# Spreading softmax divisors with two small matmuls, and moving a unit's projection beside its predecessor, in a one-core attention block

## What is computed

```python
q, k, v = heads(X @ Wq), heads(X @ Wk), heads(X @ Wv)      # 16, 8, 8 heads of 64
q, k = rope(q), rope(k)                                     # rotate by cos and sin
att = 50.0 * tanh(q @ k.T / 16 / 50.0)                      # causal mask, then softmax
y = softmax(att) @ v
x = layernorm(X + y @ Wo)
qx, s = per_token_quant_int8(x)                             # s = absmax / 127
x = layernorm(x + float16((qx @ weight.T) * s * w_scale + bias))
```

## Time and profile before

| | us |
|---|---|
| median of 3 runs | 1561.52 |
| lowest, highest | 1559.03, 1564.63 |
| the profiled execution | 1562.01 |
| its span, first to last instruction | 1560.3 |
| PE busy | 1317.1 (84%) |
| DVE busy | 1055.1 (68%) |
| ACT busy | 843.2 (54%) |
| POOL busy | 378.6 (24%) |

### The profile page before, as it was taken

How to read it: one execution, slowest core, us unless ns; L and a number is a source line. 1 busy time by engine, 2 the same in 40 slices (tenths; PEclk the granted TensorE clock), 3 DMA queues, 4 the chain that set the end, 5 groups by cost and what they waited for, 6 DMA issues and landing times.

```text
span 1560.3 us, 17566 instructions
## 1 busy us (share of the span) xinstructions
PE 1317.1 (84%) x5776; PEld 965.0 (62%) x5776; DVE 1055.1 (68%) x1334; ACT 843.2 (54%) x952; POOL 378.6 (24%) x477
## 2 busy tenths in 40 slices
PE   6489998988687999797777999979867799999564
PEld 5366776666465777575545677756655577776442
DVE  4377887763467888683456888877346788887354
ACT  4166676652227876673223877766222577788122
POOL 2231111112542111111344111111144311121354
PEclk9789999999898999899978999999999899999797
DMA  7755445366514344447621543546562344433531
GB/s 269 255 199 139 112 128 164 79 206 188 169 54 103 104 125 112 135 95 274 176 97 54 129 109 100 130 114 190 181 198 71 97 104 107 121 87 119 183 115 48
DMA packets 124715, 212.24 MB, mean 136 GB/s; under 512 B 28112, under 2 KB 70096, under 8 KB 120400
## 3 DMA queue, kind: packets, MB, share of 16 engines
q1 hardware_dynamic: 120016, 202.72, 45.7%
q10 hardware_dynamic: 4608, 8.39, 1.4%
HBM read 105.64 MB, written 38.27 MB: 92 GB/s over the span
## 4 chain that ended last, share of the span: by engine, by line
PE 48%; SPq 13%; DVE 13%; POOL 8%; DMA 7%; issue 7%; ACT 4%; POOLq 0%; DVEq 0%; ACTq 0%
PE ps L714 18%; PE ps L633 12%; PE ps L688 12%; SPq L467 7%; POOL y_raw L1256 4%; DMA rb<-r_scratch 3%; PE ps L736 3%; SPq L480 2%; PE ps L659 2%; SPq L413 1%; DVE prob_hi L1048 1%; DVE work_r L1038 1%; PE ps L756 1%; POOL rstd L1264 1%; DMA x_raw<-X_T 1%
## 5 line engine op out<-in xcount | busy, mean ns | idle before, releaser
L714 PE MATMUL ps<-prob_hi,v 128*65 128x512 f32 (+3 forms) x1280 | 419.4, 377 | 8.3 <-DVE prob_lo L1052 8.3
L688 PE MATMUL ps<-qk 128*128 128x512 f32 (+1 forms) x1280 | 328.2, 384 | 79.1 <-ACT probs L863 38.9
L863 ACT ACTIVATE probs<-ps 128x1024 f32<-128x1024 f32 x288 | 293.2, 1018 | 169.1 <-PE ps L688 167.7
L1052 DVE TENSOR_TENSOR prob_lo<-probs,prob_hi 128x1024 fp32r<-128x1024 f32 x288 | 356.6, 1238 | 9.9
L1246 POOL TENSOR_SCALAR_AFFINE_SELECT probs<-probs 128x256 f32<-128x256 f32 (+1 forms) x192 | 146.1, 768 | 829.6 <-ACT probs L868 829.6
L688 PEld LDWEIGHTS ps<-qk 128*128 128x128 f32 x1280 | 231.4, 195 | 146.1 <-issue 38.7
L868 ACT ACTIVATE probs<-probs 128x1024 f32<-128x1024 f32 x288 | 305.6, 1061 | 8.8
L633 PE MATMUL ps<-xT,w_ring 128*128 128x512 f32 x1152 | 292.5, 399 | 16.6 <-DVE xT L992 14.7
L1048 DVE CAST prob_hi<-probs 128x1024 fp32r<-128x1024 f32 x288 | 203.3, 706 | 136.5 <-POOL probs L1246 79.7
L633 PEld LDWEIGHTS ps<-xT,w_ring 128*128 128x128 f32 x1152 | 218.7, 192 | 63.4 <-DVE xT L992 15.3
L714 PE MATMUL ps<-prob_lo,v 128*65 128x512 f32 (+1 forms) x640 | 240.8, 376 | 0.0
(11 more groups left out here) (69 smaller groups left out, 982.2 us busy)
## 6 DMA issues: line engine op xcount, KB each, us to landing
qk<-work_r SPq DMA_DIRECT2D x256, 128.0 KB, 2.3
qk<-work_r SPq DMA_DIRECT2D x512, 64.0 KB, 2.0
y_scratch<-sums SPq DMA_DIRECT2D x256, 64.0 KB
wo<-wo_scratch SPq DMA_DIRECT2D x8, 2048.0 KB, 8.8
y_raw<-y_scratch SPq DMA_DIRECT2D x32, 512.0 KB, 4.3
rb<-r_scratch SPq DMA_DIRECT2D x128, 128.0 KB, 3.3
w_ring<-w_scratch SPq DMA_DIRECT2D x15, 1024.0 KB, 5.1
x_raw<-X_T SPq DMA_DIRECT2D x16, 512.0 KB, 7.2
```

Of the source, the lines that this page charges most:

```text
L688: mm = nc.tensor.matmul(scores[:, g % 2, col:col + REP * w].rearrange("p (h q) -> p h q", h=REP), qk[:, n % 2, i, 2 + part, keys], qk[:, n ...
L714: mm = nc.tensor.matmul(sums_ps[:, :, GQ - w:GQ], v[:, kt, v0:v0 + width], p[:, g % ring, col:col + REP * w].rearrange("p (h q) -> p h q", ...
L863: nc.scalar.activation(probs[:, g % PRING, :], scores[:, g % 2, :], ACT.Tanh, scale=SCORE_SCALE / SOFTCAP).then_inc(capped, 1)
L1052: nc.vector.tensor_tensor(prob_lo[:, g % PRING, :], probs[:, g % PRING, :], prob_hi[:, g % HRING, :].bitcast(F32), ALU.subtract).then_inc( ...
```

## The change

Four things move together.

1. Divisors. `invert` now also splits the inverse into a high and a low fp32r part (`inverse`, 128x32 each). `store_inverse` writes both parts to `r_scratch`, and `load_rows` loads, for one tile, four rows of 1024 numbers (two heads of a pair, high and low) onto four partitions of `rows`. A constant `spread` of 4x128 ones and zeros, made at the start, spreads them: `spread_rows` is two matmuls of 512 columns into PSUM banks 2 and 3. There is one `rows` buffer, so a tile's load waits for the spreading of the tile ahead. The broadcasting loads are gone.
2. Engines. `scale_y` goes from POOL to DVE (one 128x1024 multiply that reads PSUM), `split_y` from DVE to POOL (one 128x1024 subtraction). In the drain's lists ACT takes `keep_q` ahead of `round_y`, DVE takes `quantise` behind `rescale`, POOL takes both `inverse_std` ahead of `split_y`. The second half of Wo is loaded from ACT's queue.
3. The second unit of batches 1 to 3. Its chunks 0 and 1 leave the boundary; all three run beside unit 0, at steps 0, 5 and 9 as elsewhere. The values then use only PSUM banks 6, 7, 0, 1 in turn.
4. Beside unit 2 the chunks begin at steps 0, 3 and 6 (`turns`) instead of 0, 5 and 9, with their DVE, ACT and SP steps moved by the same amounts, and the loads of the next X are issued at step 9, not 12, ahead of `load_wq`. At the end of unit 3 `load_div` of the first quarter is at step 14 and its inversion at step 16.

```diff
         def between(m, x):
-            return m == 0 or (m % UB == 1 and m > 1 and x < 2)
+            return m == 0
...
+        def turns(u, *steps):
+
+            return tuple(s - (0, 2, 3)[x] for x, s in enumerate(steps)) if u == 2 else steps
...
-            def store_div(b, c):
-                sp.wait_ge(div_done, divs_upto(b, c))
...
+            def store_inverse(b, c):
+                sp.wait_ge(inverse_lo, divs_upto(b, c))
+                for part in range(2):
+                    sp.dma_start(r_scratch[part, 2 * c:2 * c + 2].rearrange("t h j (a n) -> (t h j a) n", n=P // G),
+                                 inverse[:, part, :].bitcast(F32)).then_inc(div_stored[c], 16)
+
+
+            def load_rows(b, t):
+                sp.wait_ge(div_stored[t // 2], 32 * (b + 1))
+                if t >= 1:
+                    sp.wait_ge(rows_spread, rows_upto(b, t - 1))
+                for part in range(2):
+                    sp.dma_start(rows[REP * part:REP * (part + 1), :].bitcast(F32),
+                                 r_scratch[part, t].rearrange("h k n -> h (k n)")).then_inc(rows_loaded, 16)
...
-                store_div(b, 2)
-                store_div(b, 3)
+                store_inverse(b, 3)
                 for t in range(NT):
                     if t == 2 and b + 1 < B:
                         sp.wait_ge(v_summed, rows_upto(b + 1, NT - 1))
...
                         load_wk(UB * b + UB + 1)
                         load_wq(UB * b + UB + 1)
-                    for i in (2 * t + 4, 2 * t + 5):
-                        if i < 2 * NT:
-                            load_rb(b, i)
+                    if t + 2 < NT:
+                        load_rows(b, t + 2)
...
+            def spread_rows(b, t):
+                if t == 0:
+                    pe.wait_ge(spread_ready, 16)
+                    pe.wait_ge(capped, scores_upto(b, NB - 1))
+                else:
+                    pe.wait_ge(y_scaled, rows_upto(b, t - 1))
+                pe.wait_ge(rows_loaded, 32 * rows_upto(b, t))
+                for e in range(2):
+                    mm = nc.tensor.matmul(ps[:, SPREAD_BANK + e, :], spread[0:2 * REP, :],
+                                          rows[0:2 * REP, e * 512:(e + 1) * 512], start=True, stop=True)
+                mm.then_inc(rows_spread, 1)
...
                 for t in range(NT):
                     if t <= 2 and more:
                         project_v(b + 1, 2 * t + 2)
                         project_v(b + 1, 2 * t + 3)
+                    if t + 1 < NT:
+                        spread_rows(b, t + 1)
...
-                if more:
-                    project(m, 0, 12, 24)
                 linear(b, NT - 2)
...
+            def scale_y(b, t):
+                dve.wait_ge(rows_spread, rows_upto(b, t))
+                dve.wait_ge(y_loaded[t % YRING], ring_upto(b, t, YRING))
...
                 for t in range(1, NT):
+                    if t + 1 < NT:
+                        scale_y(b, t + 1)
                     shift_by(b, t - 1, 0, rstd1, shift1)
-                    if t + 1 < NT:
-                        split_y(b, t + 1)
-                    quantise(b, t - 1)
                     if t >= 3:
                         stats2(b, t - 3)
                     if t >= 2:
                         rescale(b, t - 2)
                     if t >= 3:
                         shift_by(b, t - 3, 1, rstd2, shift2)
+                    quantise(b, t - 1)
                     residual1(b, t)
```

More of the change, by code:

```diff
@@ L167, in attention_block @@
         ident = over("ident", "div", [P, P], F32)
+        inverse = sb("inverse", [P, 2, P // G], F32R)
+        spread = sb("spread", [P, P], F32R)
+        spread_f32 = over("spread_f32", "prob_hi", [P, P], F32)
         ident16 = sb("ident16", [P, P], BF16)
@@ L552, in _ @@
                                 load_wq(m + 1)
-                            if u == 2 and b + 1 < B:
-                                for part in range(XU):
-                                    load_x_turned(b + 1, part)
                         if u == UB - 1 and s == 11:
```

190 lines of the change are left out of this document (86 added, 104 removed).

## The result

| us | before | after |
|---|---|---|
| median | 1564.33 (10 runs) | 1556.07 (10 runs) |
| lowest, highest | 1559.03, 1567.91 | 1550.82, 1559.72 |
| span of the profiled execution | 1560.3 | 1555.3 |

The ratio is 0.995, with a 95% interval of 0.9932 to 0.9968. The change brings 8 us, where 1489 us were forecast and 1462 to 1518 was the range: the sign was right, the size far off.

A forecast was written before the change was run, and what follows sets the result against it. It saw PE bounding unit 1 and no engine bounding the drain, where a closed round of waits took 12.14 us a tile. −18.6 − 51.4 − 10.9 + 10.5 − 2.5 = −72.9 gave 1489 us; range 1462 to 1518.

The forecast's parts named there:

- The middle of the drain: Steady tiles of the drain, residual to residual: 9.2 us a tile after the change, for 12.14 before.
- The lock: Drain: POOL's long instructions block DVE's L1114 and L1119, stretching each from under 0.5 to over 1 us.
- The boundary: Residual 7 to the next batch's first tanh: 18.2 us for 21.8, a gain of 10.9 over three.
- Unit 0: First unit of batches 1 to 3, now beside 48 projection matmuls: 52.5 us for 49, +10.5 in three.
- the 5.5 us that chunk 0's three slices should hide: Unit 0: these slices fall where PE would wait for last norms and first tanhs, so 58 − 5.5 = 52.5.
- Unit 2: Unit with chunks at earlier steps and X loaded sooner: −2.5 us over all batches.
- Net −1.5 a batch: Unit 2, three batches: 1 to 2 us sooner X against PE waits of 1.6 and 0.4; −5 to +3.
- The head: Last tanh to residual 0: −26.1 us over four batches, residual 0 coming 7.7 sooner in three, 3 in the last.
- rival A: Drain: DVE is not held up by POOL, a tile takes 7.7 us; total 1469; A and better 0.17.
- B: Projections don't hide in unit 0 (9 us) and the lock makes tiles 10.4; total 1521; chance 0.18.
- D: Drain: the spread gets its rows late in every tile, which stays near 12 us; total 1536; chance 0.05.
- the prediction's signs of being wrong: Forecast is wrong if PE's wait for rows appears in every drain tile, or if unit 0 takes 58 us.

The follow-up runs named there:

- early-X kernel: Next X's loads issued at step 11, split one step sooner, weights at step 16; on the kernel with unit 2's old steps and second-unit chunks back at the boundary: 1496.55 us.

## Why the prediction failed, step by step

**The middle of the drain: right, by its own steps.** The forecast was 9.2 a steady tile; most took 8.8, some 9.9, the last 7.9 as said (9.5 in one batch). The lock was the reason given, with L1114 and L1119 over 1 us; in the tiles around the one shown they took 0.98 to 1.55 and 1.26 to 1.37. L1114 ends 0.28 us behind POOL's subtraction and is 0.53 without it. L1127 reads PSUM and kept 0.75 beside that subtraction; a multiply of PSUM (L1020 at 97.77 in the trace before) kept 1.22 beside POOL's L1234. With both, the traces agree with the Trainium skill's page "SBUF — State Buffer", section "Who interferes with whom". The 9.9 tiles are those in which DVE waited 1.92 for PE; in the two of the last batch the granted clock was 0.83 (1489 to 1499 and 1516 to 1526 us) and PE took 1.05 us for a pair of matmuls and not 0.62, where the 8.8 tile shown has 1.00. Residual 0 to 7 came to -43.5 for -44.2, and that it came so near is partly luck: the last batch gained 13.0 for 15.6, the other three 30.4 for 28.6. In the last batch the first gaps were longer (13.7 and 9.2 for 12.5 and 8.6) and two tiles took 9.9; in the others most steady tiles were shorter than forecast.

**The boundary: right.** 18.0 us for 18.2.

**Unit 0: right mechanism, size off.** +5.0 a batch for +3.5. The failed term is the 5.5 us that chunk 0's three slices should hide: against unit 1's 58 us, 4.0 were hidden. And the move as a whole failed. With the boundary it was priced at nothing, +10.5 and -10.9; taking it back gave 11 us, of which the two marks hold 5.7, and the rest is not explained.

**Unit 2: wrong, 38 us.** The failed step is "Net −1.5 a batch", which prices what stands ahead of X and nothing that stands behind it. "they stand on SP behind `put` of chunk 1's low part" was true, and I stopped there. I did not go on to ask what now stands behind X and the two `put`s: the sums' store, whose slot ACT needs two groups later. The two waits that I did price were there (PE 1.6 us at step 3, X 1.0 for 5.3), and both were small beside the 9.8 us of the store. X in time was even priced as a gain, −5. In the last batch, which loads no X, the forecast was +2 and the unit took 9.1 more, with ACT's wait of 5.7 for the same store. I also had no price for SP's own issuing, though it is in the trace before: 16 stores a chunk, 10 us, and `SPq L467` at 7% and L480 at 2% of the chain. The two runs on unit 2 show it: 32 us come back with the old steps, 16 with one DVE order.

**The head: wrong, 29 us.** The failed step is "Residual 0 now starts at 373.46 because the broadcast holds the DVE instruction ahead of it; its `project_out` can end at about 366". That `project_out` was taken as unmoved. It starts 9.1, 6.7 and 6.1 us later in batches 0 to 2, which is 22 of the 29. Residual 0 does follow it sooner, 6.3 us behind its start and not 12.3, so the broadcast was read rightly; but the last `weigh` ahead of it now waits for DVE's roundings, these for `invert(0)`, and that for divisors whose way over DRAM the load of Wo made slow, issued 1.0 us behind the last tanh and not 15.6 as before. In the last batch residual 0 came 1.1 us sooner, not 3. `load_div(0)` and `invert(0)` a step earlier were not priced at all. Leaving Wo's low half out shortened the heads by 12 us, on the early-X kernel. How the rest divides between DVE's order, PE's low clock and the rows' round trip stays open: each attempt to shorten one lengthened another.

**The rivals.** The lock of rival A was priced at 1.5 us a tile (9.2 against 7.7); the kernel without POOL's subtraction takes 7.9 for 8.8, so 0.9 of it is shown. B had the projections' full price, D late rows in every tile. None had SP's queue in the softmax loop or the DMA engines as the bound, and the range was built of the drain's and unit 0's uncertainties; both misses lay outside them. Nor do the prediction's signs of being wrong show it: no tile waited for rows in the steady stretch, and unit 0 took 54, not 58.

## What to carry to other kernels

When a step is moved on an in-order queue, follow not only what it now stands behind but everything that now stands behind it, to the engine that needs that buffer next; and price the queue's own issue time (0.63 us a store here, 10 us a chunk). A small transfer on the critical path can be as slow as the traffic issued ahead of it (8.6 us and not 1.7 here): look at the DMA share of the stretch before a broadcast or a copy is replaced by a round trip over DRAM. And split a change of several parts: here one part was worth 3.3%, and two others gave nearly all of it back.
